# Front, first step and end of a fused graph-network kernel reordered, with the first even taps taken group by group

## The reference, cut to what matters

```
h   = relu(layernorm(x))
c1  = relu(bn1(conv1x1(h)));  cv = relu(bn2(conv17(c1)) + h)      # along the nodes, 17 taps, pad 8
s   = h @ w_se.T + b_se;  A = exp(-|s_i - s_j|^2) * adj
nmp = A @ relu(h @ w_msg.T + b_msg)
x1  = x + GRU(input=[cv, nmp], state=h)
out = x1 + (adj @ (relu(layernorm(x1)) @ weight) + bias)
```

## Time and profile before

| | us |
|---|---|
| median of 3 runs | 334.1 (333.93 to 334.57) |
| time of the profiled execution | 334.82 |
| its span in the trace | 333.0 |
| TensorE (PE) busy | 322.2 (97%) |
| VectorE (DVE) busy | 259.7 (78%) |
| ScalarE (ACT) busy | 224.1 (67%) |
| GpSimd (POOL) busy | 145.3 (44%) |

### The profile page before, as it was taken

How to read it: one execution, slowest core, us unless ns; L and a number is a source line. 1 busy time by engine, 2 the same in 40 slices (tenths; PEclk the granted TensorE clock), 3 DMA queues, 4 the chain that set the end, 5 groups by cost and what they waited for, 6 DMA issues and landing times.

```text
span 333.0 us, 6260 instructions
## 1 busy us (share of the span) xinstructions
PE 322.2 (97%) x2162; PEld 290.7 (87%) x2162; DVE 259.7 (78%) x746; ACT 224.1 (67%) x434; POOL 145.3 (44%) x128
## 2 busy tenths in 40 slices
PE   8799999989999999999999999999999999989995
PEld 5588787879889997899989998899989998889894
DVE  5788999899679977799679977789678766772475
ACT  2899668778668767687758776696767745443353
POOL 7130352139701793129801694119901594127014
PEclk9999999999999999999999999999999999999999
DMA  7902000002200131002300131001200010000003
GB/s 240 341 15 94 1 2 0 3 0 89 102 2 3 33 126 33 0 1 66 126 2 0 34 105 54 0 0 67 65 0 0 2 47 18 1 2 0 3 0 127
DMA packets 7951, 15.02 MB, mean 45 GB/s; under 512 B 1008, under 2 KB 1648, under 8 KB 7792
## 3 DMA queue, kind: packets, MB, share of 16 engines
q1 hardware_dynamic: 7776, 14.62, 12.9%
q10 hardware_dynamic: 144, 0.01, 0.0%
HBM read 10.43 MB, written 4.19 MB: 44 GB/s over the span
## 4 chain that ended last, share of the span: by engine, by line
issue 44%; POOL 30%; PE 11%; DVE 8%; ACT 4%; DMA 1%; POOLq 1%; DVEq 0%
POOL rs L1424 5%; POOL rs L1419 3%; POOL x_ring L1461 3%; POOL px L1010 3%; POOL px L1020 3%; POOL ac L1016 2%; POOL px L1013 2%; POOL base L1478 2%; POOL base L1469 2%; POOL base L1467 2%; POOL base L1475 2%; ACT hn L719 2%; DVE st L1033 1%; DMA x_ring<-x_in 1%; PE pP L328 1%
## 5 line engine op out<-in xcount | busy, mean ns | idle before, releaser
L1424 POOL TENSOR_TENSOR rs<-ve,neg_half 128x4 f32<-128x4 f32 x15 | 18.7, 1249 | 132.1 <-DVE ve L1192 132.1
L327 PE MATMUL pP<-cx_hi,conv_hi 128*128 128x256 f32 (+1 forms) x179 | 53.7, 300 | 0.0
L329 PE MATMUL pP<-cx_hi,conv_lo 128*128 128x256 f32 (+1 forms) x179 | 51.4, 287 | 0.0
L328 PE MATMUL pP<-cx_lo,conv_hi 128*128 128x256 f32 (+1 forms) x179 | 51.4, 287 | 0.0
L327 PE MATMUL pQ<-cx_hi,conv_hi 128*128 128x256 f32 (+1 forms) x139 | 41.6, 299 | 2.0 <-DVE cx_lo L1116 1.2
L329 PE MATMUL pQ<-cx_hi,conv_lo 128*128 128x256 f32 (+1 forms) x139 | 39.7, 285 | 0.0
L328 PE MATMUL pQ<-cx_lo,conv_hi 128*128 128x256 f32 (+1 forms) x139 | 39.6, 285 | 0.0
L327 PEld LDWEIGHTS pP<-cx_hi,conv_hi 128*128 128x128 f32 x179 | 33.9, 190 | 0.5
L328 PEld LDWEIGHTS pP<-cx_lo,conv_hi 128*128 128x128 f32 x179 | 33.8, 189 | 0.5
L329 PEld LDWEIGHTS pP<-cx_hi,conv_lo 128*128 128x128 f32 x179 | 33.7, 188 | 0.4
L327 PEld LDWEIGHTS pQ<-cx_hi,conv_hi 128*128 128x128 f32 x139 | 26.2, 189 | 2.6 <-issue 2.4
(11 more groups left out here) (281 smaller groups left out, 967.6 us busy)
## 6 DMA issues: line engine op xcount, KB each, us to landing
x_ring<-x_in SPq DMA_DIRECT2D x16, 256.0 KB, 2.8
adj_ring<-adj_in SPq DMA_DIRECT2D x16, 256.0 KB, 3.0
out<-x_ring SPq DMA_DIRECT2D x15, 256.0 KB, 2.0
work<-conv_in SPq DMA_DIRECT2D x1, 1088.0 KB, 7.7
x_ring<-gate_in SPq DMA_DIRECT2D x1, 576.0 KB, 8.3
out<-x_ring SPq DMA_DIRECT2D x2, 128.0 KB, 1.8
early<-early_in SPq DMA_DIRECT2D x1, 129.5 KB, 3.8
late<-late_in SPq DMA_DIRECT2D x1, 128.0 KB, 8.4
```

The source lines that it names most:

```text
L327: pe.matmul(acc, w_hi, m_hi, start=start, stop=False)
L328: pe.matmul(acc, w_hi, m_lo, start=False, stop=False)
L329: return pe.matmul(acc, w_lo, m_hi, start=False, stop=stop)
L1424: pool.tensor_tensor(rs2[g % 2][:], ve2[g % 2][:], neg_half[:, 0:GG], ALU.pow).then_inc(rs2_set, 1)
```

## The change

It edits order and waits, and a little code:

- TensorE, opening: a matmul of two zero tiles clears pQ; taps 0, 2, 4, 6 are then taken for group 0 and for group 1 by themselves (12 matmuls of 256 columns each) in place of 12 of 512 for both.
- ScalarE, opening: `place_bias(0)` ahead of `hidden_hi(1)`; `hidden_graphs(0)` and `hidden_copy(0)` from ahead of `conv1_out(0)` to behind the first splits; `round_w(0)` ahead of `conv1_out(0)`; `split_hi_first(0)` in two halves; `hidden_graphs(2)` ahead of `decay(0)`.
- VectorE, opening: `less_odd` and `split_lo_first(0)` in two halves; `split_w(0)` ahead of them and `sum_odd` behind them. Step 1: `coordinates(a)` ahead of `blend_end(qq)`, `split_lo(1, 3)` behind `right_rows(a)`, `split_lo(1, 4)` behind `pairs(b)`. Step 7: `between(t)` ahead of `shift2(qq)`.
- Ending: `keep_clock(4)` and `keep_clock(3)` are gone; GpSimd's `with_bias(14)` goes ahead of the half scales, with a wait on oT_set.

```diff
@@ TensorE
+            def even_tap_of(g, j):
+                w = (A0 + j // 2) * D
+                w_hi, w_lo = conv_hi[:, w:w + D], conv_lo[:, w:w + D]
+                cols = slice(j // 2 * GG, j // 2 * GG + QW)
+                acc = phases(0)[:, :, g]
+                x = slice(FIRST_AT[0], FIRST_AT[0] + 2)
+                m_hi, m_lo = cx_hi[:, x, g, cols], cx_lo[:, x, g, cols]
+                split_product(acc, w_hi, w_lo, m_hi, m_lo, False, False)
...
                 messages(0)
                 keep_clock(6)
+                pe.wait_ge(rows_zero, 2)
+                pe.wait_ge(c1_set, 2)
+                pe.matmul(pQ[:], left[:], right[:].rearrange("r g n -> r (g n)"), start=True, stop=False)
                 pe.wait_ge(w_split, 1)
-                pe.wait_ge(cxlo_set, 1)
-                even_tap(0)
-                even_tap(2)
-                even_tap(4)
-                even_tap(6)
+                for g in range(2):
+                    pe.wait_ge(first_lo_set, g + 1)
+                    for j in range(0, 8, 2):
+                        even_tap_of(g, j)
...
                 layer2(END - 3)
-                keep_clock(4)
                 o_turn(END)
...
                 layer2(END - 1)
-                keep_clock(3)
                 end_pass(0)
@@ ScalarE
+            def split_hi_first_of(g):
+                act.wait_ge(diff_set, g + 1)
+                act.activation(first_place(cx_hi, 0)[:, :, g], first_source(0)[:, :, g], ACT.Copy).then_inc(first_hi_set, 1)
...
                 hidden_hi(0)
+                place_bias(0)
                 hidden_hi(1)
-                place_bias(0)
-                hidden_copy(0)
-                hidden_graphs(0)
+                act.wait_ge(conv_loaded, 16)
+                round_w(0)
                 conv1_out(0)
                 conv1_out(1)
-                act.wait_ge(conv_loaded, 16)
-                round_w(0)
-                split_hi_first(0)
+                split_hi_first_of(0)
+                split_hi_first_of(1)
+                hidden_graphs(0)
+                hidden_copy(0)
...
                 first(3)
+                hidden_graphs(2)
                 decay(0)
                 left_rows(1)
-                hidden_graphs(2)
@@ VectorE
+            def less_odd_of(g):
+                dve.wait_ge(c1_set, g + 1)
+                dve.tensor_tensor(px[:, 0:2, g], c1[:, 0:2, g], c1[:, 2:4, g], ALU.subtract).then_inc(diff_set, 1)
...
                 hidden_lo(1)
+                split_w(0)
+                less_odd_of(0)
+                less_odd_of(1)
+                split_lo_first_of(0)
+                split_lo_first_of(1)
                 sum_odd()
-                less_odd()
-                split_w(0)
-                split_lo_first(0)
                 coordinates(0)
...
                 blend_start(qq)
+                shift2(pp)
                 if t == 1:
-                    split_lo(1, 3)
-                shift2(pp)
+                    coordinates(a)
                 blend_end(qq)
                 if front:
                     hidden_lo(b)
-                    coordinates(a)
+                    if t > 1:
+                        coordinates(a)
                     pair_rows(a)
                 residual(qq)
                 normalise2(qq)
-                if t == 1:
-                    split_lo(1, 4)
                 if front:
                     right_rows(a)
+                    if t == 1:
+                        split_lo(1, 3)
                     pairs(b)
+                    if t == 1:
+                        split_lo(1, 4)
+                if middle and not front:
+                    between(t)
                 shift2(qq)
                 if front:
                     masked(a)
-                if middle:
                     between(t)
@@ GpSimd, ending
                 scale2(END - 1)
+                pool.wait_ge(oT_set, END + 1)
+                with_bias(END - 1)
                 scale2_half(0)
                 pool.wait_ge(nb2_set, END + 1)
                 scale2_half(1)
                 pool.wait_ge(nb2_set, END + 2)
-                with_bias(END - 1)
                 with_bias(END)
```

More of the change, by code:

```diff
@@ L152, in gnn_kernel @@
             sem, ("st1_set", "mv1_set", "ve1_set", "rs1_set", "nb1_set", "hn_set"))
-        hn_half = sem("hn_half")
+        hn_half, first_hi_set, first_lo_set = sem("hn_half"), sem("first_hi_set"), sem("first_lo_set")
         hT_placed, hhi_set, hG_set, hT_set, hlo_set = map(sem, ("hT_placed", "hhi_set", "hG_set", "hT_set", "hlo_set"))
@@ L255, in cx_before @@
         def cx_before(t):
-            return 4 + 5 * (t - 1) if t else 0
+            return 3 + 5 * (t - 1) if t else 0
         def pre_before(t):
@@ L350, in half_rate @@
                 return last
+            def even_tap_of(g, j):
[6 more added lines that the diff above has]
+                split_product(acc, w_hi, w_lo, m_hi, m_lo, False, False)
             def even_tap(j):
-                return half_rate(pQ, 0, (A0, A2)[j % 2] + j // 2, j, start=j == 0)
+                return half_rate(pQ, 0, (A0, A2)[j % 2] + j // 2, j)
             def sum_tap(j):
@@ L544, in opening @@
                 pe.wait_ge(w_split, 4)
-                pe.wait_ge(cxlo_set, 2)
+                pe.wait_ge(cxlo_set, 1)
                 sum_tap(0)
@@ L562, in opening @@
                 sum_tap(6).then_inc(f_done[1], 1)
-                pe.wait_ge(cxlo_set, 3)
+                pe.wait_ge(cxlo_set, 2)
                 half_rate(pQ, 2, T16, 8, stop=True).then_inc(f_done[3], 1)
@@ L568, in opening @@
                 pe.wait_ge(w_split, 5)
-                pe.wait_ge(cxlo_set, 4)
+                pe.wait_ge(cxlo_set, 3)
                 pe.wait_ge(t0_set, 2)
@@ L697, in split_hi @@
                 act.activation(cx_hi[:, CX_PARTS[k][0]:CX_PARTS[k][1]], cx_source(k), ACT.Copy).then_inc(cxhi_set, 1)
+            def split_hi_first_of(g):
+                act.wait_ge(diff_set, g + 1)
+                act.activation(first_place(cx_hi, 0)[:, :, g], first_source(0)[:, :, g], ACT.Copy).then_inc(first_hi_set, 1)
             def split_hi_first(k):
-                if k in (0, 3):
-                    act.wait_ge(diff_set, 2 if k else 1)
+                if k == 3:
+                    act.wait_ge(diff_set, 3)
                 else:
@@ L752, in conv1_out @@
                     have(act, pre_set, pre_before(g // 2 - 1) + 3 if g > 2 else 0)
-                    have(act, cxlo_set, (0, 3, cx_before(g // 2 - 1) + 1)[min(g // 2, 2)])
-                    have(act, diff_set, g if g == 2 else 0)
+                    have(act, cxlo_set, (0, 2, cx_before(g // 2 - 1) + 1)[min(g // 2, 2)])
+                    have(act, diff_set, 3 if g == 2 else 0)
                 act.activation(c1[:, :, g % 2, 2 * GG:2 * GG + QW], conv1_bank(g)[:].rearrange("p (k w) -> p k w", k=PH), ACT.Relu,
@@ L1114, in split_lo_first, with split_lo_first_of @@
             def split_lo_first(k):
-                dve.wait_ge(cxhi_set, k + 1)
+                dve.wait_ge(cxhi_set, k)
                 dve.tensor_tensor(first_place(cx_lo, k), first_source(k), first_place(cx_hi, k).bitcast(F32), ALU.subtract)\
                    .then_inc(cxlo_set, 1)
-            def less_odd():
-                dve.wait_ge(c1_set, 2)
-                dve.tensor_tensor(px[:, 0:2], c1[:, 0:2], c1[:, 2:4], ALU.subtract).then_inc(diff_set, 1)
+            def less_odd_of(g):
+                dve.wait_ge(c1_set, g + 1)
+                dve.tensor_tensor(px[:, 0:2, g], c1[:, 0:2, g], c1[:, 2:4, g], ALU.subtract).then_inc(diff_set, 1)
+            def split_lo_first_of(g):
+                dve.wait_ge(first_hi_set, g + 1)
+                dve.tensor_tensor(first_place(cx_lo, 0)[:, :, g], first_source(0)[:, :, g],
+                                  first_place(cx_hi, 0)[:, :, g].bitcast(F32), ALU.subtract).then_inc(first_lo_set, 1)
             def next_less_odd():
```

## The result

The changed kernel took 336.73 us (median of 12 runs, 334.95 to 337.54), the kernel before 334.3 (12 runs): ratio 1.0065, 95% interval 1.0052 to 1.0078. Forecast was 332.2, range to 334.7. The profiled execution took 336.95 us, its span is 335.1.

What follows compares the result with a forecast made beforehand. TensorE, busy 97% of the span, was taken to bound the kernel. Opening +0.7, step 1 -0.7, step 7 -0.95 and ending -0.95 sum to -1.9: from 334.1 to 332.2 us, range 330.8 to 334.7.

Steps and rivals of the forecast that it cites:

- Opening, order: Opening: messages(0) at 15.22 and first tap at 17.7, 2.3 us late; after later waits take some up, +0.7 us.
- Opening, clock: Opening: the forecast's +0.7 us has no term for a clock fall; that stood only in rival C and rival D.
- rival C: Opening: TensorE's clock falls once, in the hole of 2.3 us, costing 1.9 us: 334.1 us; chance 0.11.
- rival D: Opening and ending: the clock falls in both places, +1.9 us in all, 336.0 us; chance 0.10.
- Step 1: 60 to 80 us: VectorE's new order makes TensorE earlier, -0.7 us kept, bounds -1.35 and -0.3.
- The -1.35 in front of distances(4): Step 1: right_rows(4) comes 1.3 us earlier on VectorE, so distances(4) moves from 71.77 to 70.4.
- the block of shift2(1): Step 1: shift2(1) may meet GpSimd's addition, holding masked(4) and between(1) up by 1.2 us, leaving -0.5 of the -0.7.
- Step 7: Step 7: between(7) runs ahead of the shift, so TensorE's wait goes: -0.95 us, bounds -0.97 and -0.5.
- Ending: Ending: o_turn(15) no longer stands behind the 8 records of keep_clock(4): -0.95 us, bounds -1.05 and -0.4.
- Sum: Whole kernel: +0.7 - 0.7 - 0.95 - 0.95 = -1.9 us, from 334.1 to 332.2 us.

## Why the prediction was wrong, step by step

- **Opening, order: right in mechanism.** messages(0) forecast at 15.22, was 15.26 (15.05 at full clock); the first tap forecast at 17.7, was 17.62 at full clock; gaps taken up as worked out; +0.65 for +0.7, where one execution stands against one and executions differ by 1 us there.
- **Opening, clock: the step that failed.** The sum had no term for it, all opening costs were worked out at the full clock. It stood only as rival C, with a chance of 0.11 and a price of 1.9, and as one of the two falls of rival D (0.10). It happened in every run of the changed kernel. Where it lasted long, as in 9 of its 12 runs, its price is 2.4 to 3.0: 336.3 less 333.4 and 336.06 less 333.03 in runs of two kernels, 2.95 and 2.4 in two pairs of traces. Filling the hole won back 2.5. With step 1 at its measured +0.55 and no fall the forecast would have been 333.5, inside the range: the fall alone takes the time out of it. The chance was too small because I compared the single hole of 2.3 with the longest of before (1.23); what TensorE did from 9 to 15 us was 2.60 us of work in 6, in short bursts between two new waits (0.94 and 2.32). Whether the length of a hole counts, or how little TensorE works around it, no run here separates. The price was too small because it was taken from the extra time of the first 3.8 us; here TensorE had enough work queued to be slow until 21 us.
- **Step 1: wrong sign.** The -1.35 in front of distances(4) came (-1.2). I then let TensorE keep 0.7, as att(5) ended at 82.19 and it came at 82.94. I had not asked what else `neighbour_sums(5)` waits for: it fills the bank that `sums_lo(4)` reads, and n_lo(4) came right behind att(5), at 82.11 to 82.79. Nothing could be kept: the term is -0.7 for +0.55. That left the block of shift2(1), which I had named but priced at 0.2; it costs 0.55, as VectorE was the bound. The two runs with and without it show both (+0.55, 0). The shift itself is 1.1 longer (1.26 for 0.16). Half of that came back because a later VectorE operation of before, which ended with another GpSimd addition, now comes when GpSimd is free (0.17 for 0.80); with the block away it takes 0.78 again. Three lines of before, n_lo(4) among them, and the last of after:

```profile
77.26 1.29 POOL L1469 TENSOR_TENSOR base<-base,s 128x512 f32<-128x512 f32 x1
77.78 0.80 DVE L1040 TENSOR_SCALAR ve<-mv 128x8 f32<-128x8 f32 x1
82.11 0.68 DVE L1112 TENSOR_TENSOR n_lo<-pF,n_hi 128x512 fp32r<-128x512 f32 x1
82.58 0.17 DVE L1054 TENSOR_SCALAR ve<-mv 128x8 f32<-128x8 f32 x1
```

The Trainium skill's rule on the shared port pair ("SBUF — State Buffer", "Who interferes with whom") named the right operations: the shift has two SBUF inputs, and it ended with GpSimd's addition at 78.2. In step 7 after the change, between(7), with one input in PSUM, took 0.75 beside such an addition (1.30 from 301.62), as by that rule.
- **Step 7: right**, -1.0 for -0.95. **Ending: right**, -0.8 up to the last end_layer2 and -1.0 to the span's end, for -0.95, though not by every step of the working: the second shift was still late, and the four activations kept a wait inside (1.74 for 1.79, not 1.65).
- **Rival D** has the number nearest to the result, 336.0, and that is chance: its second fall, in the ending, did not happen in any of the 11 runs with only the fillers out. What stands in its place is a longer first fall and a loss at step 1. In the changed kernel TensorE is busy 25.00 of 25 us from 300 to 325.
- **Sum:** with the measured terms, +0.65 + 2.95 + 0.55 - 1.0 - 1.0 = +2.15, which is the difference of the two profiled executions (+2.13) as it must be, since the terms are parts of it. The medians say +2.4.

## What to carry to other kernels

Before a wait is put in front of short matmuls, look at all that TensorE does around it, not only at the longest hole; where it is short bursts between waits, as in this opening, take the lower clock as a likely case and price it by what is queued behind the wait, at twice its time (here messages(0) took 2.11 for 1.16). When an engine that bounds a stretch only gets its work in another order, nothing behind the last reordered instruction gets earlier, so list every semaphore of the next instructions, buffer releases too, before a gain is carried on. In this kernel fillers could be dropped from the ending, with dense work just ahead (no fall in 11 runs), and one more set of them in the opening's hole was worth 2.5 us. To place a gain or a loss of half a microsecond, compare distances between two instructions of one trace; here they repeat within 0.1 us where the start of a stage moves by 1.

## What was not expected of the hardware

- The same kernel, on the same chip, fell for a long time, a short one or not at all: mean clock 0.99, 0.995 or 1.0, at 336.1, 334.8 and 333.0 us for the kernel with place_bias(0) back. So a profile of one execution can show any of them; the list of clocks of all runs belongs beside it.
- With the later hole filled, the clock still fell in 3 of 12 runs. The one that was profiled fell behind the hole of 1.1 us ahead of conv1(1), before the fillers. With step 1 back, a hole of the same size (1.06) did nothing in the profiled run. In the kernel before, where conv1(1) follows conv1(0) closely, none of 77 runs fell.
- TensorE's lower level at the start of the kernel lasts differently from run to run: the same 16 records took 1.95 to 3.06 us.
